# Expert rows transposed by a DMA on ScalarE's queue instead of on TensorE, and later issue of three experts' first weight loads

## The chip, the cores and the metric

One Trainium2 chip, one core of it. The metric is the device time of the whole program in microseconds; three runs of the kernel before gave 1927.49, 1928.22 and 1937.55, median 1928.22.

## The reference, cut to what matters

Two transformer layers over 2048 tokens of 512 features. The first has a latent attention and a mixture of experts, the second a memory attention and an MLP with a key-indexed expert table. Only the mixture of experts is touched by the change:

```python
h = x.reshape(T, d)                                   # 2048 x 512, normalized
scores = softmax(h @ gate_w.T)                        # 16 experts
topk_w, topk_idx = top_k(scores, 6)
cw = zeros((T, E)).at[arange(T)[:, None], topk_idx].add(topk_w)
for e in range(E):                                    # w_gate, w_up: 352 x 512, w_down: 512 x 352
    out = silu(h @ w_gate[e].T) * (h @ w_up[e].T) @ w_down[e].T
    y = y + cw[:, e:e + 1] * out
```

## The kernel before

Every fp32 product is made of three fp16 products (`mm3`, lines 234 to 236: high by high, high by low, low by high).

**Before the experts.** The attention runs for some 575 us. Beside it the kernel splits the expert weights into fp16 halves in DRAM (`wsp`), normalizes the 16 tiles of 128 tokens, stores each as a row table (`rows`, 2112 bytes a token: 512 high and 512 low halves and the 16 gate weights), stores the residual into `xacc`, and writes each token's number into the lists of its six experts (`recs`) with 96 indirect DMAs of GpSimd (L2226).

**The expert loop** runs over `NBLK` = 111 blocks of up to 128 tokens, each block of one expert. For block b:

- GpSimd gathers the block's 128 rows from `rows` into `xb[:, b % 6]` (`gather_rows`, L2298), `ROWS_AHEAD` = 5 blocks ahead: its loop is gather(b+5), then wait for `y_cp` of b and for `summed` of b-1, then the indirect DMA that adds the block's result to `xacc` (L2311). Since two of these could add to the same row, each waits until the one before it has landed.
- TensorE transposes the rows (`turn_rows`, 8 transposes of 128x128 fp16 into bank 4, L1061), ScalarE copies the bank to `xT[:, b % 2]` (`rows_copy`, L1468), and TensorE computes gate and up (`expert_up`, 24 matmuls of 352 columns).
- ScalarE takes the silu (L1474), VectorE multiplies (L2060), ScalarE and VectorE make the high and low halves (L1480, L2065), TensorE transposes them (`turn_hidden`, L1088), VectorE copies (L2072), TensorE computes the down product (`expert_down`, 9 matmuls of 512 columns), ScalarE scales it into one of `YB` = 3 buffers (`rows_out`, L1487) and increments `y_cp`. `rows_out` of b waits until the addition of b-3 has landed.
- TensorE's order in one turn of the loop is up(b+1), turn_rows(b+2), turn_hidden(b), down(b-1). ScalarE's is rows_out(b-2), silu(b+1), rows_copy(b+2), hidden_high(b+1).
- SyncE loads weights into four slots (`load_a`: 1408 KB gate and up, `load_d`: 768 KB down); at each block it issues a load that is carried out only where an expert is finished (L747, L755, with `cond`). It also reads the token lists, four blocks at a time (`records`, L714), and loads the memory for the next layer, 256 KB every third block (`memory_load`, L737).

**The start of the loop on SyncE** (L698 to L770): after the last head product it issues the gate and up weights of expert 0, the down weights of experts 0, 1 and 2, and, after the last attention product, the gate and up weights of expert 1. Then it waits for the tables, the stores of `xacc` and `rows`, and all 96 list writes (L759 to L764), reads the first list (L765) and the next seven (L714), and issues the rest of the first four experts' weights.

Of the kernel before, what the change touches and what calls it, by code (L numbers as in the profile page):

```python
# [10 lines left out]
ACT = mybir.ActivationFunctionType  # L11
# [35 lines left out]
XB, YB = 6, 3  # L47
REC_BATCH, REC_RING, ROWS_AHEAD = 4, 5, 5
# [11 lines left out]
def build(nc, ins, out):  # L60
    with ExitStack() as ctx:
# [3 lines left out]
        def sem(name):  # L65
            return ctx.enter_context(nc.semaphore(name))
# [388 lines left out]
        def pieces_of(m):  # L455
# [18 lines left out]
        xT = er2.take(2, 8 * P, dt=F16)  # L474
# [8 lines left out]
        assert er2.at <= xrow_at  # L483
        x_flat = x[:, :, :].rearrange("p a b -> p (a b)")
# [10 lines left out]
        xt_mm, xt_cp, e_g, e_u, e_sg, e_m, e_hh, e_hl, ht_mm, ht_cp, e_y, y_cp, e_cw = (  # L495
            sem(f"e_{what}") for what in ("xt_mm", "xt_cp", "g", "u", "sg", "m", "hh", "hl", "ht_mm", "ht_cp", "y",
# [123 lines left out]
        def _(sp):  # L620
# [79 lines left out]
            for e in range(SLOTS - 1):  # L700
                first_d(e)
            sp.wait_ge(y_mm, STEPS)
            first_a(1)
# [61 lines left out]
            sp.dma_start(rid[:, 0:1], recs[0:P, :]).then_inc(first_list, 16)  # L765
            records(0)
            records(1)
            first_a(2)
            first_d(3)
            first_a(3)  # L770
# [43 lines left out]
        def _(pe):  # L814
# [240 lines left out]
            def turn_rows(b):  # L1055
                pe.wait_ge(xb_in[b % XB], 16 * (b // XB + 1))
                if b > 0:
                    pe.wait_ge(xt_cp, b)
                o = bank[4][:, :].bitcast(F16)
                for i in range(8):  # L1060
                    m = pe.transpose(o[:, i * P:(i + 1) * P], xb[:, b % XB, i * P:(i + 1) * P], id16[:, :])  # L1061
                m.then_inc(xt_mm, 1)

# [3 lines left out]
            def expert_up(b, slot):  # L1067
                pe.wait_ge(xt_cp, b + 1)
                if b >= 2:
                    pe.wait_ge(e_m, b - 1)  # L1070
                pe.wait_ge(load_a[b % SLOTS], 16 * (b // SLOTS + 1))
                base = pe.snap(slot * (2 * AW))
                for i, done in ((0, e_g), (1, e_u)):
                    o = bank[2 * i + b % 2][:, 0:MOE_D]
                    for d in range(DC):
                        hi, lo = (wa[:, ds(base + (4 * d + 2 * k + i) * MOE_D, MOE_D)] for k in range(2))
                        m = mm3(pe, o, xT[:, b % 2, d * P:(d + 1) * P], xT[:, b % 2, (DC + d) * P:(DC + d + 1) * P],
                                hi, lo, start=(d == 0), stop=(d == DC - 1))
                    m.then_inc(done, 1)
# [27 lines left out]
            turn_rows(0)  # L1107
            turn_rows(1)
            expert_up(0, slots[0])
            for b in range(NBLK - 3):  # L1110
                expert_up(b + 1, slots[b + 1])
                slots[b + 2] = slot_of(b + 2)
                turn_rows(b + 2)
                turn_hidden(b)
                if b > 0:
                    expert_down(b - 1, slots.pop(b - 1))
# [3 lines left out]
            turn_rows(NBLK - 1)  # L1120
# [119 lines left out]
        def _(act):  # L1240
# [223 lines left out]
            def rows_copy(b):  # L1464
                act.wait_ge(xt_mm, b + 1)
                if b >= 2:
                    act.wait_ge(e_u, b - 1)
                act.activation(xT[:, b % 2, :], bank[4][:, :].bitcast(F16), ACT.Copy).then_inc(xt_cp, 1)  # L1468
# [21 lines left out]
            rows_copy(0)  # L1490
            rows_copy(1)
            expert_silu(0)
            hidden_high(0)
            for b in range(NBLK - 1):
# [5 lines left out]
                if b + 2 < NBLK:  # L1500
                    rows_copy(b + 2)
# [673 lines left out]
        def _(pool):  # L2175
# [111 lines left out]
            def gather_rows(b):  # L2287
# [7 lines left out]
                if b >= XB:  # L2295
                    pool.wait_ge(xt_mm, b - XB + 1)
                    pool.wait_ge(e_cw, b - XB + 1)
# [138 lines left out]
```

## Time and profile before

| | |
|---|---|
| median of three runs | 1928.22 us |
| the profiled execution, its own time | 1926.74 us |
| its span, first to last instruction | 1925.0 us |
| TensorE (PE) busy | 1801.6 us, 94% |
| VectorE (DVE), ScalarE (ACT), GpSimd (POOL) busy | 1093.7, 884.7, 820.2 us |
| mean granted TensorE clock | 0.977 |

The page gives busy time by engine, the span in forty slices, the DMA queues, and the chain of work that ended last. A busy share over the whole span says little here, since the program has stages with different limits; the expert loop lies between 606 and 1330 us. The time of a matmul in the profile is longer than its distance from the next one, as they are pipelined, so distances between starts are used where TensorE's pace matters. For a DMA the profile gives its issue on the engine and, for some, the time from issue to landing.

### The profile page before, as it was taken

What the parts mean: (1) busy time and instruction counts of PE and PEld (TensorE: products, weight loads), DVE (VectorE), ACT (ScalarE), POOL (GpSimd) and SP (SyncE); (2) the same over time, 40 slices, a digit from 0 to 9 for tenths busy, and PEclk for the clock granted to TensorE, in tenths of its full rate; (3) what the DMA queues carried; (4) which work ended last, traced back from release to release, by engine and by line L of the source; (5) the groups of instructions that cost most, each with busy time, mean ns of one, the idle gap of its engine ahead of it and who ended that gap; (6) DMA issues with size and microseconds to landing.
All of it is one profiled execution on the core that took longest, in us unless ns stands there. A gap on an engine that the chain in (4) does not pass through costs nothing.

```text
span 1925.0 us, 39526 instructions
## 1 busy us (share of the span) xinstructions
PE 1801.6 (94%) x12786; PEld 1073.8 (56%) x12789; DVE 1093.7 (57%) x2985; ACT 884.7 (46%) x1833; POOL 820.2 (43%) x731
## 2 busy tenths in 40 slices
PE   6989999999972999999999999995899999999998
PEld 3566666766631666666666666663554444444444
DVE  4578888888852323322322323223656877777776
ACT  4588888888841443444434434433732221122111
POOL 4234456656664344443433443442112444544442
PEclk9999999999985999999999999998999999999999
DMA  8255587777776666766665765545012355555653
GB/s 310 88 163 175 178 164 168 186 178 170 182 161 166 159 147 145 160 163 152 146 150 135 165 153 100 93 82 129 33 35 66 125 187 202 206 171 210 203 178 143
DMA packets 137921, 294.81 MB, mean 153 GB/s; under 512 B 39200, under 2 KB 64416, under 8 KB 133600
## 3 DMA queue, kind: packets, MB, share of 16 engines
q1 hardware_dynamic: 86752, 157.47, 29.5%
q0 software_dynamic: 46368, 126.29, 26.7%
q10 hardware_dynamic: 4608, 8.52, 1.5%
q8 instruction: 115, 1.88, 0.4%
q14 instruction: 78, 0.64, 0.1%
HBM read 426.00 MB, written 78.33 MB: 262 GB/s over the span
## 4 chain that ended last, share of the span: by engine, by line
PE 81%; DVE 6%; DMA 4%; issue 4%; ACT 3%; POOL 1%; SPq 0%; another core or an unknown queue 0%; ACTq 0%; POOLq 0%; DVEq 0%
PE bank L234 21%; PE bank L236 21%; PE bank L235 21%; PE bank L1061 3%; PE bank L1088 2%; PE bank L851 1%; DVE work_arena L1578 1%; DMA x_sum<-x,work_arena 1%; PE bank L927 1%; ACT xt_arena L1314 1%; PE bank L842 1%; POOL expert_tokens L2226 1%; DMA work_arena<-in_ctxT 1%; DMA work_arena<-in_pk_w 1%; DMA work_arena<-in_moe_w 1%
## 5 line engine op out<-in xcount | busy, mean ns | idle before, releaser
L234 PE MATMUL bank<-work_arena,xt_arena 128*128 x1221 | 404.7, 331 | 2.8 <-DVE xt_arena L2072 1.9
L235 PE MATMUL bank<-work_arena,xt_arena 128*128 x1221 | 404.6, 331 | 0.0
L236 PE MATMUL bank<-work_arena,xt_arena 128*128 x1221 | 404.5, 331 | 0.0
L2311 POOL DMA_INDIRECT x_sum<-x,work_arena x111 | 176.5, 1590 | 392.5 <-DMA x_sum<-x,work_arena 222.9
L2060 DVE TENSOR_TENSOR xt_arena<-xt_arena,bank 128x352 f32<-128x352 f32 x111 | 57.9, 522 | 405.9 <-PE bank L236 373.0
L234 PE MATMUL bank<-work_arena 128*128 128x512 f16 (+1 forms) x600 | 226.3, 378 | 15.1 <-DVE x L1883 6.8
L235 PE MATMUL bank<-work_arena 128*128 128x512 f16 (+1 forms) x600 | 226.4, 379 | 0.0
L236 PE MATMUL bank<-work_arena 128*128 128x512 f16 (+1 forms) x600 | 226.3, 378 | 0.0
L1468 ACT ACTIVATE xt_arena<-bank 128x1024 f16<-128x1024 f16 x111 | 113.6, 1023 | 224.4 <-PE bank L1061 212.0
L234 PE MATMUL bank<-xt_arena,work_arena 128*128 128x512 f16 x528 | 200.1, 379 | 1.7 <-DVE xt_arena L194 1.7
L235 PE MATMUL bank<-xt_arena,work_arena 128*128 128x512 f16 x528 | 200.1, 379 | 0.0
L236 PE MATMUL bank<-xt_arena,work_arena 128*128 128x512 f16 x528 | 200.1, 379 | 0.0
L2318 POOL TENSOR_TENSOR work_arena<-work_arena 128x512 f16<-128x512 f32 x64 | 73.3, 1164 | 267.7 <-ACT work_arena L1453 267.7
L236 PEld LDWEIGHTS bank<-work_arena,xt_arena 128*128 128x128 f16 x1221 | 119.7, 98 | 85.1
L234 PEld LDWEIGHTS bank<-work_arena,xt_arena 128*128 128x128 f16 x1221 | 119.8, 98 | 82.6 <-issue 3.3
L235 PEld LDWEIGHTS bank<-work_arena,xt_arena 128*128 128x128 f16 x1221 | 119.7, 98 | 79.4
L2327 POOL DMA_INDIRECT work_arena<-in_pk_e,work_arena x128 | 135.0, 1055 | 36.7 <-issue 33.4
L2298 POOL DMA_INDIRECT x<-token_rows,work_arena x111 | 112.0, 1009 | 49.7 <-issue 27.7
L1578 DVE SCALAR_TENSOR_TENSOR work_arena<-work_arena 128x704 f16<-128x704 f32 (+2 forms) x90 | 89.9, 1001 | 70.8 <-ACT work_arena L1361 54.1
L2212 POOL TENSOR_TENSOR xt_arena<-xt_arena,work_arena 128x512 f32<-128x512 f32 x64 | 66.8, 1043 | 137.0 <-DVE work_arena L1668 133.9
L1314 ACT ACTIVATE xt_arena<-xt_arena,work_arena 128x128 f32<-128x128 f32 x256 | 123.2, 482 | 2.1
L1487 ACT ACTIVATE x<-bank,xt_arena 128x512 f32<-128x512 f32 x111 | 76.3, 687 | 99.6 <-PE bank L236 92.6
(278 smaller groups left out, 3823.0 us busy)
## 6 DMA issues: line engine op xcount, KB each, us to landing
work_arena<-expert_w SPq DMA_DIRECT2D x111, 1408.0 KB
work_arena<-expert_w SPq DMA_DIRECT2D x111, 768.0 KB
work_arena<-in_moe_w SPq DMA_DIRECT2D x64, 352.0 KB
expert_w<-work_arena SPq DMA_DIRECT2D x64, 352.0 KB
work_arena<-in_moe_w SPq DMA_DIRECT2D x64, 192.0 KB
expert_w<-xt_arena SPq DMA_DIRECT2D x64, 192.0 KB
work_arena<-in_mlp_w SPq DMA_DIRECT2D x8, 1536.0 KB
work_arena<-in_head_w SPq DMA_DIRECT2D x16, 512.0 KB, 5.6
```

The costliest lines, as they stand in the source:

```text
L234: pe.matmul(o, a_hi, b_hi, start=start, stop=False)
L235: pe.matmul(o, a_hi, b_lo, start=False, stop=False)
L236: return pe.matmul(o, a_lo, b_hi, start=False, stop=stop)
L1314: last = act.activation(prob[:, m % 3, i, :], prob[:, m % 3, i, :], ACT.Exp, bias=ebias[:, m % 4, i:i + 1], scale=seg_scale[:, t:t + 1], a ...
L1468: act.activation(xT[:, b % 2, :], bank[4][:, :].bitcast(F16), ACT.Copy).then_inc(xt_cp, 1)
L1487: act.activation(ysb[:, b % YB, :], bank[6 + b % 2][:, :], ACT.Copy, scale=ecw[:, b % 4, :]).then_inc(y_cp, 1)
L1578: return dve.scalar_tensor_tensor(out=o, in0=src, scalar=scale, in1=hi, op0=ALU.mult, op1=ALU.subtract)
L2212: pool.tensor_tensor(prob[:, m % 3, :, :], prob[:, m % 3, :, :], rinv[:, m % 4, :].unsqueeze(2).to_broadcast([P, 4, P]), ALU.mult).then_in ...
L2298: pool.indirect_dma_start(out=xbu[:, b % XB, :], out_offset=None, in_=rows[:, :], in_offset=bass.IndirectOffsetOnAxis(ap=rid[:, i:i + 1], ...
L2311: pool.indirect_dma_start(out=xacc[:, :], out_offset=bass.IndirectOffsetOnAxis(ap=rid[:, i:i + 1], axis=0), in_=ysb[:, b % YB, :], in_offs ...
L2318: pool.tensor_tensor(h_lo[:, S_ % 2, c, :], m2[:, c, :], h_hi[:, S_ % 2, c, :], ALU.subtract).then_inc(hlo, 1)
L2327: pool.indirect_dma_start(out=gbuf[:, n % 2 * SETS + i - FIRST[n], :], out_offset=None, in_=ins["pk_e"][:, :], in_offset=bass.IndirectOffs ...
```

## The change

The eight transposes per block on TensorE and ScalarE's copy go. In their place ScalarE issues, for each block, one DMA that transposes the 128 x 1024 fp16 rows of `xb` into `xT` (256 KB, from SBUF to SBUF), three blocks ahead; `xT` has four buffers instead of two. ScalarE's instruction stream waits for the gather of that block (`xb_in`), for the up product that last read the buffer, and for the transposing DMA before the last one. TensorE waits for `xt_in` instead of `xt_cp`. In GpSimd's loop the gather waits for `xt_in` instead of `xt_mm`.

On SyncE only expert 0's weights (2176 KB) are issued ahead of the wait for the lists; experts 1, 2 and 3 follow behind the first list, between the further lists.

```diff
+XT_SLOTS, TURN_AHEAD = 4, 3
-        xT = er2.take(2, 8 * P, dt=F16)
+        xT = er2.take(XT_SLOTS, 8 * P, dt=F16)
...
             first_a(0)
-            for e in range(SLOTS - 1):
-                first_d(e)
-            sp.wait_ge(y_mm, STEPS)
-            first_a(1)
+            first_d(0)
...
             sp.dma_start(rid[:, 0:1], recs[0:P, :]).then_inc(first_list, 16)
+            first_a(1)
             records(0)
+            first_d(1)
+            first_a(2)
             records(1)
-            first_a(2)
+            first_d(2)
+            first_a(3)
             first_d(3)
-            first_a(3)
...
             def expert_up(b, slot):
-                pe.wait_ge(xt_cp, b + 1)
+                pe.wait_ge(xt_in[b % 2], 16 * (b // 2 + 1))
...
-            turn_rows(0)
-            turn_rows(1)
             expert_up(0, slots[0])
             for b in range(NBLK - 3):
                 expert_up(b + 1, slots[b + 1])
                 slots[b + 2] = slot_of(b + 2)
-                turn_rows(b + 2)
                 turn_hidden(b)
...
-            def rows_copy(b):
-                act.wait_ge(xt_mm, b + 1)
+            def rows_turned(b):
+                act.wait_ge(xb_in[b % XB], 16 * (b // XB + 1))
+                if b >= XT_SLOTS:
+                    act.wait_ge(e_u, b - XT_SLOTS + 1)
                 if b >= 2:
-                    act.wait_ge(e_u, b - 1)
-                act.activation(xT[:, b % 2, :], bank[4][:, :].bitcast(F16), ACT.Copy).then_inc(xt_cp, 1)
+                    act.wait_ge(xt_in[b % 2], 16 * (b // 2))
+                act.dma_start(xT[:, b % XT_SLOTS, :].rearrange("p (c r) -> p c r", c=8), xb[:, b % XB, 0:8 * P],
+                              transpose=True).then_inc(xt_in[b % 2], 16)
...
-            rows_copy(0)
-            rows_copy(1)
+            for b in range(TURN_AHEAD):
+                rows_turned(b)
...
                 expert_silu(b + 1)
-                if b + 2 < NBLK:
-                    rows_copy(b + 2)
+                if b + TURN_AHEAD < NBLK:
+                    rows_turned(b + TURN_AHEAD)
                 hidden_high(b + 1)
...
                 if b >= XB:
-                    pool.wait_ge(xt_mm, b - XB + 1)
+                    pool.wait_ge(xt_in[b % 2], 16 * ((b - XB) // 2 + 1))
                     pool.wait_ge(e_cw, b - XB + 1)
```

## Rows read from the trace of the kernel before

**Rows 1.** The page: span, and busy time of each engine.

```profile
span 1925.0 us, 39526 instructions
PE 1801.6 (94%) x12786; PEld 1073.8 (56%) x12789; DVE 1093.7 (57%) x2985; ACT 884.7 (46%) x1833; POOL 820.2 (43%) x731
```

**Rows 2.** A stretch: PE, PEld, DVE, ACT, POOL busy, clock, DMA share, GB/s.

```profile
700.00:800.00 100.00, 100.00 (x748) 63.61 (x747) 34.55 (x84) 40.63 (x64) 42.78 (x32) 1.00 0.67 150
```

**Rows 3.** Timeline of one block: start, duration, operation, [idle before, releaser].

```profile
900.71 0.46 ACT L1474 ACTIVATE xt_arena<-bank 128x352 f32<-128x352 f32 x1 [1.10 <-PE bank L236]
...
902.30 0.61 PE L1061 MATMUL bank<-id,x 128*128 128x128 f16 x8
...
902.75 0.50 PE L1088 MATMUL bank<-id,xt_arena 128*128 128x128 f16 x6
903.07 1.02 ACT L1468 ACTIVATE xt_arena<-bank 128x1024 f16<-128x1024 f16 x1 [1.90 <-PE bank L1061]
...
907.01 0.46 ACT L1474 ACTIVATE xt_arena<-bank 128x352 f32<-128x352 f32 x1 [1.10 <-issue]
```

**Rows 4.** The additions into x_sum, and what ended GpSimd's idle time before them.

```profile
L2311 POOL DMA_INDIRECT x_sum<-x,work_arena x111: 1541/1583/2516, 635.1 to 1325.0; - x111
  DMA x_sum<-x,work_arena: 222.9, 66
  ACT x L1487: 146.5, 41
DMA to landing us min/median/max: 3.7/4.9/11.9
```

**Rows 5.** Timeline of GpSimd: the first addition and three later ones.

```profile
635.11 1.63 POOL L2311 DMA_INDIRECT x_sum<-x,work_arena  x1 [14.16 <-ACT x L1487]
...
654.02 1.57 POOL L2311 DMA_INDIRECT x_sum<-x,work_arena  x1 [3.43 <-ACT x L1487]
...
663.40 1.60 POOL L2311 DMA_INDIRECT x_sum<-x,work_arena  x1 [6.51 <-issue]
...
668.91 1.59 POOL L2311 DMA_INDIRECT x_sum<-x,work_arena  x1 [2.62 <-DMA x_sum<-x,work_arena]
```

**Rows 6.** Weight load, memory load; landings of the additions of 1183.57 and 1189.87.

```profile
653.09 0.35 SPq L747 DMA_DIRECT2D work_arena<-expert_w  x1
...
1183.56 0.62 SPq L737 DMA_DIRECT2D work_arena<-in_ctxT  x1
DMA to landing us min/median/max: 5.4/5.4/5.4
...
DMA to landing us min/median/max: 4.8/4.8/4.8
```

**Rows 7.** Stretches between additions: memory load, none, memory load (columns as Rows 2).

```profile
1183.57:1189.87 6.30, 6.30 (x49) 4.01 (x47) 1.86 (x5) 2.56 (x4) 2.56 (x2) 1.00 0.60 127
1189.87:1196.18 6.31, 6.31 (x49) 4.01 (x47) 1.86 (x5) 2.56 (x4) 2.57 (x3) 1.00 0.46 87
...
1202.48:1208.79 6.31, 6.31 (x49) 4.01 (x47) 1.86 (x5) 2.56 (x4) 2.57 (x3) 1.00 0.66 130
```

**Rows 8.** Waits of SyncE's queue, then the timeline of the loop's start.

```profile
SPq L763 <- DMA token_rows<-xt_arena: 29.1, 1, 29.1
594.89 0.97 POOL L2226 DMA_INDIRECT expert_tokens<-work_arena  x1 [0.30 <-issue]
606.14 0.34 SPq L765 DMA_DIRECT2D work_arena<-expert_tokens  x1
612.35 0.97 POOL L2298 DMA_INDIRECT x<-token_rows,work_arena  x1 [1.21 <-DMA work_arena<-expert_tokens]
613.58 1.03 PE L1061 MATMUL bank<-id,x 128*128 128x128 f16 x8 [20.97 <-DMA x<-token_rows,work_arena]
615.82 1.01 PE L1061 MATMUL bank<-id,x 128*128 128x128 f16 x8 [1.21 <-DMA x<-token_rows,work_arena]
616.63 0.50 PE L234 MATMUL bank<-work_arena,xt_arena 128*128 x1
```

More of the change, by code:

```diff
@@ L483, in build @@
         assert er2.at <= xrow_at
+        er2.at = (er2.at + 7) // 8 * 8
+        xT = er2.take(XT_SLOTS, 8 * P, dt=F16)
         x_flat = x[:, :, :].rearrange("p a b -> p (a b)")
@@ L494, in build @@
         xb_in = [sem(f"xb_in{s}") for s in range(XB)]
-        xt_mm, xt_cp, e_g, e_u, e_sg, e_m, e_hh, e_hl, ht_mm, ht_cp, e_y, y_cp, e_cw = (
-            sem(f"e_{what}") for what in ("xt_mm", "xt_cp", "g", "u", "sg", "m", "hh", "hl", "ht_mm", "ht_cp", "y",
+        xt_in = [sem(f"xt_in{s}") for s in range(2)]
+        e_g, e_u, e_sg, e_m, e_hh, e_hl, ht_mm, ht_cp, e_y, y_cp, e_cw = (
+            sem(f"e_{what}") for what in ("g", "u", "sg", "m", "hh", "hl", "ht_mm", "ht_cp", "y",
                                           "y_cp", "cw"))
@@ L1053, in _ @@
             last.then_inc(q_mm, 1)
[L1055 to L1062, printed above, removed]
             def slot_of(b):
@@ L1076, in expert_up @@
                         hi, lo = (wa[:, ds(base + (4 * d + 2 * k + i) * MOE_D, MOE_D)] for k in range(2))
-                        m = mm3(pe, o, xT[:, b % 2, d * P:(d + 1) * P], xT[:, b % 2, (DC + d) * P:(DC + d + 1) * P],
+                        m = mm3(pe, o, xT[:, b % XT_SLOTS, d * P:(d + 1) * P],
+                                xT[:, b % XT_SLOTS, (DC + d) * P:(DC + d + 1) * P],
                                 hi, lo, start=(d == 0), stop=(d == DC - 1))
@@ L1119, in _ @@
             slots[NBLK - 1] = slot_of(NBLK - 1)
-            turn_rows(NBLK - 1)
             turn_hidden(NBLK - 3)
```

## The prediction

> **What bounds the kernel now.** I read the page first, for the shares [rows 1]; then the busy time by stretch, since the shares are a mean over stages; then one block of the expert loop in the timeline; then, because the change adds traffic, the waits and landings of the other chain that runs block by block, GpSimd's additions. TensorE is busy for 94% of the span, and in the loop it never stops: 100.00 us of 100 at a granted clock of 1.00, the 2.4 GHz level, while the DMA engines are at 0.67 [rows 2]. One block lasts from one silu to the next, 900.71 to 907.01, 6.30 us [rows 3]. So TensorE sets the loop's pace, and what the change takes off TensorE seems to be a gain in full.
>
> The reader should look at who is second. The additions into x_sum follow each other one at a time, each waiting for the landing of the last. The first is issued at 635.1 and the last at 1325.0: 110 intervals in 689.9 us, a mean of 6.27. Of GpSimd's idle times before them 66 were ended by the landing of the addition before (with 4 more put down to others), 41 by ScalarE's result [rows 4]. In well over half of the blocks the chain of additions, not TensorE, is the later of the two. It is elastic: it falls behind when a weight load is carried out and catches up after. Behind the load issued at 653.09 the interval from 654.02 to 663.40 is 9.38 us, and the next, 663.40 to 668.91, is 5.51 [rows 5, 6]. In that interval GpSimd was idle for 2.62, so its own work (this issue, its gaps and the next gather) is 5.51 - 2.62 = 2.89 us. About 5.5 us is the chain's floor: a landing of 4.9 [rows 4] and some 0.6 from there to the next issue.
>
> **The change part by part.**
>
> *TensorE loses eight transposes per block.* Their first starts at 902.30 and the next work at 902.75, 0.45 us, so a block would take 6.30 - 0.45 = 5.85 us [rows 3]; over 111 blocks 50 us. ScalarE's copy of 1.02 us goes too [rows 3]; ScalarE's four instructions take 2.66 us of 6.30, so this frees nothing on the path.
>
> *What is late next: the additions.* How fast can that chain go as it is? The 41 waits ended by ScalarE sum to 146.5 us [rows 4]; without the first, 14.16 [rows 5], they are 132.3 over 40 intervals, and with 2.86 of work each these 40 last 247 us. At the floor of 5.5 they would last 220. So with TensorE infinitely fast the additions still need 689.9 - 27 = 663 us. Of the 50 us at most 27 can come through, and that is with nothing added to the chain.
>
> *What a transposing DMA adds to it.* It moves 256 KB a block on the same 16 engines. No DMA here transposes. The nearest rows are the memory loads, also 256 KB, issued by an engine's hardware queue. The one at 1183.56 goes out with the addition of 1183.57: that addition lands after 5.4 us, the next, with no load beside it, after 4.8 [rows 6], so 0.6 us more; the DMA share of the stretches is 0.60 and 0.66 with such a load and 0.46 without, that is 0.14 x 6.3 = 0.9 to 0.20 x 6.3 = 1.3 us of all 16 engines per transfer [rows 7]. From below the bound is zero: an addition's transfer can be over before the other starts. A gain is excluded, since nothing is taken off the DMA engines. From above it is the whole 1.3 us. The phase decides. Once the additions are behind, ScalarE at its transposing DMA of block b+3 waits for the gather of b+3, which GpSimd issues 1.9 us after addition b-3; a gather took 615.82 - 612.35 = 3.47 us to its user [rows 8], which makes 5.4 after that addition, right where the next is issued. That is the phase of the row with 0.6 and not that of a load that falls between two. I take 0.45, nearer to that row than to zero, since a copy within SBUF doesn't read DRAM. The chain then needs 663 + 110 x 0.45 = 712.5 us against 689.9: +23 us. It breaks even at 27 / 110 = 0.24 us per block.
>
> Here the Trainium skill speaks for the change: Advanced Engine Details and Errata, X-Bar Transpose (TRN2), says that transposing DMAs run about as fast as plain ones, at 350 to 400 GB/s. An estimate from it is 262144 B / 375 GB/s = 0.7 us of all engines, a little under the rows' 0.9 to 1.3; scaling the 0.6 us by it gives 0.4 us a block and a chain of 663 + 44 = 707 us, +17.
>
> *ScalarE's queue.* Behind a DMA whose gather is late stand hidden_high and the next rows_out. The copy starts at 903.07, and TensorE transposes the hidden halves that follow it one block after 902.75, at 909.05 [rows 3]; the copy's 1.02 us and two halves of about 0.5 us lie between, which leaves more than 3 us, so waits up to that are covered. An ordinary 256 KB issue takes 0.36 to 0.62 us of a queue [rows 6]; if a transposing one takes up to the 3.6 us that ScalarE has free (6.30 - 2.66), the block is still covered. `xt_in` instead of `xt_mm` in GpSimd's loop concerns a block six back: nothing. The doubled `xT` costs nothing. With expert loads in flight the transposing DMA shares the engines with them and lands late too; it is issued more than a block, 5.8 us, before its user, which covers a delay like the 3.9 us of 9.38 against 5.5.
>
> *The start.* The last list write is issued at 594.89, the first list read only at 606.14; SyncE waited for the store of the row table [rows 8]. Some 2.9 MB of weights (768 + 768 + 1408 KB) were in front. If writes land in 3 us, the list can be read at 598: -8 us at most. Against it: these loads now run beside the first gathers and transposes, and records stand behind 1408 KB. From 606.14 to the first up product it is 10.5 us; the first gather's user starts at 613.58 and the two PE transposes and copies end at 616.63, 3.05 us, which the first transposing DMA takes over at about the same price [rows 8]. Beside a weight load an addition took 3.9 more; I take 2.5 for the gather and 2.5 for the transposing DMA. -8 + 5 = -3 us, bounds -8 and +5.
>
> *The sum*, against the profiled time of 1926.74: +23 - 3 = +20, 1946.7. The median of the runs is 1.5 above that execution: 1948.
>
> **The rivals.**
>
> 1. *TensorE's gain comes through*: the transposing DMA falls into the pause between two additions, as after 1.9 us of GpSimd's own work, when no transfer of it is in flight. Between 0 and 0.19 us a block; the chain needs 663 to 684, the loop gains 27 to 6, the start 3 to 8. About 1928 - 20 - 6 = 1902. For it: the pause is some 2 us long and the added transfer 0.9 to 1.3. Against: the phase above.
> 2. *They cancel*: 0.19 to 0.37 us a block; 1919 to 1938, about 1928.
> 3. *The additions are slowed by 0.45*, the forecast, 1938 to 1965: the other side of rival 1, one mechanism, deciding from 0.24 us on.
> 4. *The DMA engines fill up*. Now 0.67 x 6.3 = 4.2 us of 16 engines a block in the stretch with loads [rows 2]; if a transposing transfer takes 2.7 us, twice the costlier memory load, a block needs 6.9 us there, and with some 90 such blocks +55 us, and queueing on top: 1980 to 2020. It decides from 6.3 - 4.2 = 2.1 us on. No row shows a 256 KB transfer that slow.
> 5. *The transposing DMA doesn't pipeline*: its queue handles it in pieces, eight of 128 x 128, and it takes longer than a block. Each piece at 1.2 us, the cost of a whole memory load, gives 9.6 us a block, 111 x 3.3 = +366 us, 2290. Against it: all 256 KB transfers here take a tenth of that. The Trainium skill has a rule of this kind, against the change: VectorE: DVE Perf Modes, The three transpose paths, gives 1309 ns for one 128x128 by DMA against 390 on TensorE and advises TensorE; eight in a row would make, as an estimate, 10.5 us a block and 2390. Its 390 ns is not what this trace shows on TensorE, 0.45 us for all eight [rows 3].
>
> **How the numbers follow.** Rival 1: 0.27. Rival 2: 0.18. Forecast 3: 0.35. Rival 4: 0.13. Rival 5: 0.07. A difference under 0.5%, 9.6 us, can't be told from no change here. So faster 0.27, same 0.18, slower 0.55. The time is that of case 3, 1948, whose own range is 1938 to 1965. The range for 8 in 10 goes down to 1898, leaving out a little of rival 1, and up to 2020, leaving out rival 5.
>
> **What would show it.** In the profile after: no L1061; 24 + 6 + 9 matmuls a block with gaps between them, TensorE below 100 of 100 in the loop; nearly all of GpSimd's idle time before L2311 ended by the landing of x_sum, ScalarE's share of it almost gone; quiet intervals near 6.0 instead of 5.5; a landing median of about 5.3 instead of 4.9; the DMA share of the loop above 0.8; the first list read near 598. I'd be wrong if the landing stays at 4.9 and TensorE is still full (rival 1), if the DMA share is at 1 (rival 4), or if ScalarE's queue shows issues of several microseconds or TensorE waits for `xT` in every block (rival 5).

## The result and the profile after

The changed kernel takes 1997.13 us (median of 4 runs, 1984.20 to 2009.36) against 1929.74 us for the kernel before on the same chip: 1.034 times as long, 95% interval 1.030 to 1.038. The forecast was 1948 us, so the sign was right and the rise was over three times as large as forecast, +67 us instead of +20. The four executions lie 25 us apart, those of the kernel before 10 us, and the profiled one is the fastest of the four, 1984.20 us.

The page of the changed kernel: span, busy times, DMA queues, two parts of the chain that ended last, and the two groups of additions and first products.

```profile
span 1982.4 us, 37643 instructions
PE 1775.6 (90%) x11901; PEld 1026.3 (52%) x11901; DVE 1084.7 (55%) x2985; ACT 770.1 (39%) x1722; POOL 820.3 (41%) x731
...
q1 hardware_dynamic: 86752, 157.47, 28.8%
q0 software_dynamic: 46368, 126.29, 26.2%
q10 hardware_dynamic: 121824, 37.63, 11.5%
...
PE 43%; DMA 32%; issue 9%; DVE 7%; ACT 4%; POOL 2%; SPq 1%; another core or an unknown queue 1%; ACTq 1%; POOLq 0%; DVEq 0%
...
L235 PE MATMUL bank<-work_arena,xt_arena 128*128 x1221 | 411.2, 337 | 95.7 <-DMA xt_arena<-x 93.3
```

TensorE is busy for 26 us less [rows 1] and yet the span is 57 us longer. A third of the chain that ended last is now DMA time. The queue q10, ScalarE's, carried 4608 packets in the kernel before, all but a few of them ahead of the loop; with the transposing DMAs it carries 121824 and takes 11.5% of the DMA engines' span.

The stretch of [rows 2], three more of the loop, and its greater part (PE, PEld, DVE, ACT, POOL busy, clock, DMA share, GB/s):

```profile
640.00:1180.00 540.00, 480.39 (x3066) 282.67 (x3064) 144.79 (x398) 118.28 (x236) 199.46 (x154) 0.97 0.88 176
700.00:800.00 100.00, 91.54 (x582) 53.54 (x583) 31.60 (x79) 21.65 (x46) 38.26 (x30) 0.98 0.86 182
800.00:900.00 100.00, 84.32 (x531) 49.37 (x530) 25.43 (x72) 22.22 (x44) 36.90 (x29) 0.94 0.89 182
1100.00:1200.00 100.00, 85.17 (x545) 50.35 (x544) 24.83 (x70) 21.64 (x42) 35.04 (x28) 0.95 1.00 174
1200.00:1300.00 100.00, 99.25 (x661) 60.00 (x659) 30.12 (x85) 26.53 (x51) 43.65 (x34) 1.00 0.83 145
```

GpSimd issues twice per block, a gather and an addition. From 1200 on, where few weights are loaded, x34 makes 17 blocks in 100 us, 5.9 us each: faster than before's 6.3, as the change intends. Between 800 and 900 x29 makes 14.5 blocks, 6.9 us each, and from 1100 to 1200, with 7.1 us a block, the times of all packets add up to all of the 16 engines' time (share 1.00). In the queue's row of that stretch 3.67 MB are 14 transposing DMAs, and they took 37.0 us of 16 engines, 2.64 us each:

```profile
q10 hardware_dynamic: 14761, 3.67, 37.0%
```

The additions into x_sum, as [rows 4], and the transposing DMA: issue durations, first and last start, who waited.

```profile
L2305 POOL DMA_INDIRECT x_sum<-x,work_arena x111: 1541/1583/1627, 647.1 to 1380.5; - x111
  DMA x_sum<-x,work_arena: 323.5, 84
  ACT x L1481: 41.0, 6
DMA to landing us min/median/max: 3.9/5.3/12.0
...
L1461 ACTq DMA_TRANSPOSE xt_arena<-x x111: 1247/1252/6562, 616.6 to 1353.2; - x111
  PE bank L235: 93.3, 25
```

84 waits for the landing of the addition before instead of 66, 6 for ScalarE instead of 41: the chain of additions has taken TensorE's place. Where a wait is for several things at once, the profile can name the wrong one, so I also set each addition beside the landing of the one before and the end of ScalarE's result for it. In the changed kernel the landing came last in 97 of 110 intervals, in the kernel before in 70. The profiled executions differ in three terms. The first addition comes at 647.1 instead of 635.1: +12. The loop takes 1380.5 - 647.1 = 733.4 us instead of 689.9: +43.5. What follows takes 601.9 instead of 600.0: +2. Together +57.5, and the median lies another 10 or so above.

### The profile page after: what moved, and what is told of

It is laid out like the page before. It is cut to its first block, busy times and chain, and to the rows that moved or that the text cites. A ratio compares the mean times of both kernels' runs of the same rounds, so it can differ in the third digit from the quotient of the medians.

```text
span 1982.4 us, 37643 instructions
## 1 busy us (share of the span) xinstructions
PE 1775.6 (90%) x11901; PEld 1026.3 (52%) x11901; DVE 1084.7 (55%) x2985; ACT 770.1 (39%) x1722; POOL 820.3 (41%) x731
## 3 DMA queue, kind: packets, MB, share of 16 engines
q1 hardware_dynamic: 86752, 157.47, 28.8%
q10 hardware_dynamic: 121824, 37.63, 11.5%
## 4 chain that ended last, share of the span: by engine, by line
PE 43%; DMA 32%; issue 9%; DVE 7%; ACT 4%; POOL 2%; SPq 1%; another core or an unknown queue 1%; ACTq 1%; POOLq 0%; DVEq 0%
DMA x_sum<-x,work_arena 25%; PE bank L235 11%; PE bank L237 11%; PE bank L236 11%; DMA x<-token_rows,work_arena 3%; DVE work_arena L1572 2%; PE bank L854 1%; DMA xt_arena<-x 1%; ACT xt_arena L1305 1%; PE bank L930 1%; DMA expert_w<-work_arena 1%; PE bank L845 1%; POOL expert_tokens L2220 1%; DMA work_arena<-in_pk_w 1%; DVE xt_arena L1572 1%
## 5 line engine op out<-in xcount | busy, mean ns | idle before, releaser
L235 PE MATMUL bank<-work_arena,xt_arena 128*128 x1221 | 411.2, 337 | 95.7 <-DMA xt_arena<-x 93.3
L236 PE MATMUL bank<-work_arena,xt_arena 128*128 x1221 | 410.6, 336 | 0.0
L237 PE MATMUL bank<-work_arena,xt_arena 128*128 x1221 | 410.2, 336 | 0.0
L1474 ACT ACTIVATE xt_arena<-xt_arena 128x352 f16<-128x352 f32 x111 | 55.1, 496 | 470.9 <-issue 399.6
L235 PEld LDWEIGHTS bank<-work_arena,xt_arena 128*128 128x128 f16 x1221 | 121.3, 99 | 192.0 <-issue 112.8
L2059 DVE TENSOR_TENSOR xt_arena<-xt_arena 128x352 f16<-128x352 f32 x111 | 58.3, 525 | 294.4 <-ACT xt_arena L1474 283.2
L237 PEld LDWEIGHTS bank<-work_arena,xt_arena 128*128 128x128 f16 x1221 | 121.5, 99 | 84.1
L236 PEld LDWEIGHTS bank<-work_arena,xt_arena 128*128 128x128 f16 x1221 | 121.2, 99 | 80.2 <-issue 0.4
```

Source lines behind the costliest of these rows:

```text
L235: pe.matmul(o, a_hi, b_hi, start=start, stop=False)
L236: pe.matmul(o, a_hi, b_lo, start=False, stop=False)
L237: return pe.matmul(o, a_lo, b_hi, start=False, stop=stop)
L2059: dve.tensor_tensor(eh_lo[:, b % 2, 0:MOE_D], em[:, b % 2, :], eh_hi[:, b % 2, 0:MOE_D], ALU.subtract).then_inc(e_hl, 1)
```

## The experiments

Ratios are to runs of the kernel before on the same chip in the same comparison, with the 95% interval; times are medians. "+" lines of an edit are cut to the core. A loop is the time from the first addition's issue to the last one's, 689.9 us before.

**The changed kernel again.** No edit.

> The changed kernel itself, for comparison with the others of this set: 1.030 to 1.040, with executions as far apart as before, some 25 us.

2003.73 us, 1.040 [1.036, 1.043]. The size holds: +3.4 to +4.0% in two comparisons. Its profiled execution is one of the long ones, 2011.3 us span, with a loop of 761.3 us instead of 733.4, the mean granted clock at 0.956 and TensorE's waits for the turned rows in the loop at 75.5 us.

**The start.** The changed kernel with the old order of weight loads, and the kernel before with the new one.

```diff
-            first_d(0)
+            for e in range(SLOTS - 1):
+                first_d(e)
+            sp.wait_ge(y_mm, STEPS)
+            first_a(1)
```

> The changed kernel with the old order of the first weight loads on SyncE (three down loads and expert 1's up load ahead of the lists). In the changed kernel the first list is read at 601.4 instead of 606.1, but the first up product starts at 629.9 instead of 616.6, since the first three transposing DMAs take 14.4 us to issue beside the weight loads. Theory start (the loads moved behind the list delay the first transposing DMAs): first up product at 617 to 621 and 9 to 13 us less in total, about 1985 against the changed kernel's median of 1997. Rival (the transposing DMA is slow by itself, loads or not): first up product still near 630 and the total within 3 us of 1997.

> The kernel before with only the new order of the first weight loads; transposes stay on TensorE. Theory start: without transposing DMAs the order costs little, the first list is read at about 601 and the first up product starts between 612 and 618; the total is 1922 to 1932 against 1930. Rival (the weight loads behind the list delay the gathers themselves): first up product at 620 or later and 1935 or more.

2005.39 us, 1.033 [1.024, 1.042], and 1926.75 us, 1.002 [1.000, 1.004]. The order of loads by itself does nothing to the time: its first list is read at 600.08, but its first product starts at 618.50, 1.9 us later than before. In the changed kernel undoing it makes no difference that the scatter would let through. What the start costs is seen in the timeline of the changed kernel (start, duration, operation, [idle before, releaser]):

```profile
593.14 0.97 POOL L2220 DMA_INDIRECT expert_tokens<-work_arena  x1 [0.30 <-issue]
...
601.41 0.34 SPq L765 DMA_DIRECT2D work_arena<-expert_tokens  x1
...
607.76 2.64 POOL L2292 DMA_INDIRECT x<-token_rows,work_arena  x1 [13.65 <-DMA work_arena<-expert_tokens]
...
616.62 14.43 ACTq L1461 DMA_TRANSPOSE xt_arena<-x  x3
...
629.86 0.47 PE L235 MATMUL bank<-work_arena,xt_arena 128*128 x1 [38.99 <-DMA xt_arena<-x]
```

The list is read 4.7 us earlier (601.41 against 606.14, [rows 8]), and the first product starts 13.2 us later (629.86 against 616.63). Between them stand 14.43 us from ScalarE's first transposing DMA to the end of its third. With the old order the three take as long, but the first product starts at 612.51, before the later rows are turned:

```profile
606.73 16.21 ACTq L1461 DMA_TRANSPOSE xt_arena<-x  x3
```

These rows merge three instructions and the waits between them. Taken apart, the changed kernel's three issues, and those of the spare plain copy in runs of 256 B described below (shortest, median and longest, first and last start):

```profile
L1461 ACTq DMA_TRANSPOSE xt_arena<-x x3: 1248/1422/6562, 616.6 to 629.8; - x3
...
L1498 ACTq DMA_DIRECT2D xt_arena<-x x3: 602/685/853, 619.3 to 633.9; - x3
```

The third may go out only when the first has landed. The first transposing DMA landed at 629.7, 13.1 us after its issue, and then both the third goes out and the first product starts. The plain copy landed 14.5 us after its issue. So the one issue of 6.56 us is peculiar to the transposing DMA, but not the late landing, which decides when the first product starts.

**Is the chain of additions the bound?** The additions alternate between two sums in DRAM, so that each waits for the one before the last; once in the changed kernel, once in the kernel before with one transpose per block in place of eight, and that one also with a single sum. None of the three computes the reference: the second sum is left out of the output, and with one transpose most of `xT` keeps the rows of the first two blocks.

```diff
-                for i in range(8):
+                for i in range(8 if b < 2 else 1):
...
-                if b > 0:
-                    pool.wait_ge(summed, 16 * b)
+                if b > 1:
+                    pool.wait_ge(summed[b % 2], 16 * (b // 2))
...
+                    out=(xacc, xacc_b)[b % 2][:, :], out_offset=bass.IndirectOffsetOnAxis(ap=rid[:, i:i + 1], axis=0),
```

> The changed kernel with the additions of even and odd blocks going to two different sums, each addition waiting for the one before the last; the second sum is left out of the output. This takes the chain of additions off the path and leaves all traffic. Theory additions (the forecast's: the chain of additions is the bound): the waits of TensorE for xT mostly go too, the loop falls from 733 to 680 to 695 us and the total to 1945 to 1960. Theory late rows (transposing DMAs land late beside weight loads, TensorE waits for xT, and ScalarE's queue waits behind them): TensorE still waits 70 us or more for xT and the total stays above 1980.

> The kernel before with one transpose of the eight and a copy of 128 columns in every block from the third on (the rest of xT keeps the rows of the first two blocks, so the output is another). No transposing DMA, no added traffic. The forecast's step: the additions let through at most 27 of TensorE's 50 us. So 1895 to 1905 against 1926. Rival (the chain of additions has no say while TensorE is faster): TensorE's 0.39 us times 109 in full, 1880 to 1886.

> The same with the additions of even and odd blocks going to two sums (the second is left out of the output), so that each waits for the one before the last. If the additions are what holds the kernel with one transpose back, this one gains the rest: 1878 to 1888. If both are equal, the chain of additions was not the bound.

One transpose: 1916.89 us, 0.993 [0.990, 0.995]. One transpose and two sums: 1886.26 us, 0.976 [0.973, 0.980]. The changed kernel with two sums: 1955.70 us, 1.018 [1.013, 1.024], its four executions from 1928.49 to 1964.66, so that its size is known roughly only. The kernel with one transpose, its additions and a wait in its loop:

```profile
L2312 POOL DMA_INDIRECT x_sum<-x,work_arena x111: 1541/1583/1927, 633.6 to 1317.3; - x111
  DMA x_sum<-x,work_arena: 251.8, 75
  ACT x L1488: 90.9, 25
...
PEld bank L1061 <- DMA x<-token_rows,work_arena: 27.2, 18, 4.3
```

Seven of eight transposes are 44 us by the forecast's price. With two sums 46 us come through (1932.18 - 1886.26), so that price is right. With one sum it is 15. The loop falls from 689.9 to 683.7 us only, and in the loop TensorE now waits for gathered rows, which it never did before: a late addition holds up the gather that GpSimd issues behind it. The chain of additions is the bound as soon as TensorE gets faster. (Two sums in the kernel before with all eight transposes weren't run; TensorE is busy for 100 us of 100 there.)

The 25 waits put down to ScalarE mislead here. The k-th of ScalarE's results (L1488) belongs to the k-th addition. The addition of 856.70 uses the result of 849.54, which was ready 6.5 us earlier. The addition before it, of 851.00, landed after 4.9 us, and 0.8 us later the next went out:

```profile
849.54 0.69 ACT L1488 ACTIVATE x<-bank,xt_arena 128x512 f32<-128x512 f32 x1 [1.22 <-PE bank L236]
851.00 1.58 POOL L2312 DMA_INDIRECT x_sum<-x,work_arena  x1 [2.95 <-ACT x L1488]
855.46 0.69 ACT L1488 ACTIVATE x<-bank,xt_arena 128x512 f32<-128x512 f32 x1 [1.23 <-DMA x_sum<-x,work_arena]
856.70 1.58 POOL L2312 DMA_INDIRECT x_sum<-x,work_arena  x1 [2.83 <-ACT x L1488]
...
DMA to landing us min/median/max: 4.9/4.9/4.9
```

Set beside each other in this way, the landing came last in 108 of the 110 intervals. The whole loop of 683.7 us is the chain: 595.6 us of landings, 87.1 us from a landing to the next issue (0.77 us in most), and 1.0 us of waiting for ScalarE.

In the changed kernel the two sums give back some 31 to 42 us (1.018 against 1.034 and 1.040), and more by its fastest execution. Behind them the next limits stand (windows of that execution, columns as above):

```profile
800.00:900.00 100.00, 98.07 (x653) 59.06 (x651) 29.10 (x82) 26.06 (x50) 42.51 (x33) 1.00 1.02 208
1000.00:1100.00 100.00, 97.23 (x635) 58.25 (x633) 28.88 (x83) 26.50 (x50) 42.38 (x33) 0.98 1.00 186
```

At 6.1 us a block the DMA share is 1.00 and TensorE is busy for 97 to 98 us of 100; TensorE alone would need 5.85.

**The wait or the traffic?** The kernel before, with ScalarE waiting for the gather of block b+3 and nothing else; then with an unused DMA of the gathered rows per block in the changed kernel's place, which transposes, copies in runs of 256 B, or copies in runs of 2048 B. Besides, ScalarE waits for the spare DMA before the last, as in the changed kernel, and GpSimd's gather for that of six blocks back; the kernel with the wait alone has neither.

```diff
+            def rows_spare(b):
+                act.wait_ge(xb_in[b % XB], 16 * (b // XB + 1))
...
+                act.dma_start(spareT[:, b % 4, :].rearrange("p (c r) -> p c r", c=8), xb[:, b % XB, 0:8 * P],
+                              transpose=True).then_inc(spare_in[b % 2], 16)
```

> The kernel before with only the wait of the change in ScalarE's stream: before hidden_high it waits for the gather of three blocks ahead; no DMA is added. Theory queue (ScalarE's waiting in order for a gather that is issued behind a late addition costs time by itself): 1940 or more, with 200 us or more of ScalarE's idle time ended by the gather. Theory contention: the wait alone costs under 5 us, 1924 to 1931, since TensorE has slack for the hidden halves.

> The kernel before (transposes on TensorE, old start) with one transposing DMA per block added on ScalarE's queue, at the same place as in the changed kernel, into a spare buffer that nobody reads. Pure added traffic and queue time, no gain. Theory contention (the transposing DMA makes the additions and gathers late, whoever uses its result): the total is 1970 to 2010, as in the changed kernel, and the landing median of the additions 5.3 to 5.7. Theory late rows (a large part of the loss is TensorE waiting for xT): the total is 1935 to 1960.

> The same as the kernel with the spare transposing DMA, but the spare DMA is a plain copy of the same 256 KB in runs of 256 bytes. Theory packets (the cost is the 1024 packets of 256 bytes, some 25 ns each on an engine): within 10 us of the kernel with the spare transposing DMA. Rival (the transposition itself is what costs): under 1940.

> The same with the plain copy in runs of 2048 bytes, 128 packets. Theory packets: some 0.7 us of 16 engines a block instead of 1.6; the forecast's own kind of transfer. With TensorE still doing the transposes the additions have 27 us of room over the loop, so the total is 1925 to 1940. Rival (bytes are what counts): as with 256-byte runs, 1960 or more.

| added to the kernel before | us | ratio | loop, us | per block | of 16 engines, each |
|---|---|---|---|---|---|
| wait alone | 1932.06 | 1.000 [0.998, 1.001] | | | |
| copy, 2048 B runs | 1960.30 | 1.019 [1.017, 1.021] | 717.8 | +0.25 | 0.73 us |
| copy, 256 B runs | 1969.40 | 1.021 [1.018, 1.023] | 722.6 | +0.30 | 1.2 us |
| transposing DMA | 2009.83 | 1.042 [1.038, 1.047] | 741.7 | +0.47 | 1.90 us |

"Per block" is the loop's growth over 110 intervals, in the profiled execution. For the transposing DMA that is the fastest of six (1984.37 us), for the copies the fastest (2048 B) and the slowest (256 B) of five, so the last row's +0.47 is low beside its median. The last column comes from the DMA queues in the stretch 1200 to 1300: the share of 100 us over the transfers in it, which are 16 by their bytes and 15.5 for the transposing DMA; q10 of the three kernels in the table's order of copies, then the transposing one:

```profile
q10 hardware_dynamic: 2304, 4.20, 11.7%
```

```profile
q10 hardware_dynamic: 16656, 4.20, 19.5%
```

```profile
q10 hardware_dynamic: 16356, 4.07, 29.5%
```

The wait for the gather costs nothing. Any 256 KB beside the chain, with the waits that come with it, costs about 2% (the expectation for runs of 2048 B was under 1%), and that the rows are transposed on the way doubles it: at the same bytes and nearly the same packets (16656 and 16356) the packets take half as long again, and the issue takes a median of 1.25 us of ScalarE's queue instead of 0.60, and 10.5 us at worst:

```profile
L1498 ACTq DMA_TRANSPOSE xt_arena<-x x111: 1247/1249/10547, 610.5 to 1359.4; - x111
```

The landings of the additions grow nearly alike: 638.2 us over the loop with the transposing DMA, 630.5 and 625.6 with the copies in runs of 256 and 2048 B, 583.3 before. What differs more is TensorE's wait for the hidden halves, the first of which ScalarE makes behind its DMA. With the transposing DMA and with the copy in runs of 256 B, in the loop:

```profile
PE bank L1092 <- DVE xt_arena L2080: 28.8, 26, 2.7
```

```profile
PE bank L1092 <- DVE xt_arena L2079: 14.4, 14, 1.2
```

It is 13.6 us with runs of 2048 B and 1.7 with the wait alone. So of the 19 us between the first two loops 8 go with longer landings and 14 with ScalarE's late halves; the two overlap in part, and neither was changed by itself.

**Half of it.** The same spare DMA with 128 KB; and a working mixture, in which TensorE turns the high halves (four transposes) and a DMA the low halves.

```diff
+                act.dma_start(spareT[:, b % 4, 0:4 * P].rearrange("p (c r) -> p c r", c=4), xb[:, b % XB, 0:4 * P],
+                              transpose=True).then_inc(spare_in[b % 2], 16)
```

> The kernel before with a spare transposing DMA of 128 KB per block, half of the full one. If engine time is the cost, it is like the plain copy of 256 KB in runs of 2048 bytes, which takes about as much engine time: ratio 1.012 to 1.022. If the transposition costs beyond its engine time (the half change with TensorE's saving gave 1.028): 1.028 to 1.040.

> The kernel before with half of the change: the high halves are transposed by TensorE (4 transposes, a copy of 512 columns), the low halves by a transposing DMA of 128 KB three blocks ahead; old start. TensorE saves 0.22 us a block, 25 us. Theory additions: the chain has 27 us of room and the half transfer costs it about half of the full one; 1920 to 1945. Theory late rows: TensorE waits for the low halves beside each weight load, 1955 or more.

1969.74 us, 1.024 [1.020, 1.028], and 1977.62 us, 1.028 [1.026, 1.030]. Half the bytes cost 2.4%, which is about half of the whole's 4.2 or a little more, and lies between the two ranges expected. The mixture gains nothing over the spare: 25 us less of TensorE's work (half of the 50) don't show.

**Where no weights are in flight.** Transposing DMAs for the last 21 blocks only.

```diff
+                if b >= LATE:
+                    return
```

> The kernel before with the change's transposing DMAs for the last 21 blocks only, where hardly any weight load is left; old start. In the changed kernel the intervals between additions there are 5.5 to 6.5 us, some 5.95 in the mean, against 6.30 before. If the additions' floor plus 0.3 to 0.4 us per transposing DMA holds: a gain of 4 to 9 us, 1917 to 1922. If the transposing DMA costs its 0.64 us a block here too: 1926 or slower.

1930.96 us, 0.999 [0.996, 1.002], loop 686.5 us. The 4 to 9 us of gain that were expected don't show beyond the scatter; the loop is 3.4 us shorter. Where the DMA engines were at about half, the change costs nothing. The loss is made beside the weight loads.

**Shorter runs of the weight loads.** Those loads in runs of 1408 and 1536 B (q1 then has 107232 packets instead of 86752), in the changed kernel and in the kernel with the spare transposing DMA.

```diff
+                             max_dma_last_dim=1408).then_inc(load_a[e], 16)
...
+                             max_dma_last_dim=1536).then_inc(load_d[e], 16)
```

> The changed kernel with the expert weight loads cut into runs of 1408 and 1536 bytes instead of rows of 11264 and 6144 bytes; same bytes, same order. Theory packets in turn (a DMA engine takes packets of the queues in turn, so that a transposing DMA's 256-byte packets each wait for one of 11264 bytes): the intervals of 11 us between additions beside a weight load fall to 8 or 9, TensorE's wait for xT from 93 us to under 40, the first three transposing DMAs issue in under 8 us instead of 14.4, and the total falls by 20 to 45 us, to 1950 to 1975. Rival (bytes, not packets, are what is shared): nothing changes by more than 5 us, or it is slower for the smaller runs.

> The kernel before with the spare transposing DMA of 256 KB per block, and the expert weight loads in runs of 1408 and 1536 bytes. If what makes the transposing DMA cost twice the plain copy (1.042 against 1.0205) is its packets' waiting behind long weight packets: 1.020 to 1.030. If it is its own time on the engines or the way it goes through them: 1.036 to 1.045.

1977.43 us, 1.024 [1.017, 1.031], and 1996.98 us, 1.034 [1.030, 1.038]. Both lie below the kernels without the edit: the first by 1.0 to 1.6 of a per cent (1.034 and 1.040), the second by 0.8 (1.042). The intervals overlap or touch, but for that against 1.040. That the long runs of the weights hold up the others may be a fifth to two fifths of the cost; it isn't the main part. The transposing DMA itself took no less of the engines: 1.9 us between 640 and 1180 with the spare one, with and without the edit.

**The lead.** The changed kernel with the rows turned two blocks ahead instead of three.

```diff
-XT_SLOTS, TURN_AHEAD = 4, 3
+XT_SLOTS, TURN_AHEAD = 4, 2
```

> The changed kernel with TURN_AHEAD = 2 instead of 3: ScalarE no longer waits for the gather three blocks ahead, but the transposing DMA has a block less until its user. Theory late rows: TensorE's wait for xT grows from 93 us to 150 or more and the total by 10 to 30 us. Theory queue: ScalarE's waits fall and the total falls by 10 us or more. Theory additions and traffic: within 8 us of the changed kernel in the same set of runs.

2133.51 us, 1.107 [1.103, 1.110]: 130 us over the changed kernel. Its transposing DMA with who waited, its additions with what ended GpSimd's idle time, and one window:

```profile
  PE bank L235: 212.4, 82
...
L2305 POOL DMA_INDIRECT x_sum<-x,work_arena x111: 1541/1583/1627, 649.1 to 1532.5; - x111
  ACT x L1481: 498.3, 89
  DMA x_sum<-x,work_arena: 74.2, 17
...
640.00:1180.00 540.00, 426.99 (x2567) 244.47 (x2566) 122.01 (x334) 108.04 (x197) 166.84 (x130) 0.93 0.74 145
```

TensorE waits in 82 blocks instead of 25, for 212 us instead of 93, and the additions wait for its results 89 times. The DMA share falls to 0.74, so full engines aren't the reason here: one block less of lead no longer covers the transfer. Issued behind the silu of b+1, it has less than a block until TensorE's up product of b+2. In its chain of waits one such transfer reads

```profile
796.87 5.75 DMA xt_arena<-x
```

5.75 us, nearly a block. The changed kernel with the old order, in a long execution, has the landings of all 111:

```profile
DMA to landing us min/median/max: 2.7/5.3/23.5
```

The granted clock of the stretch is 0.93; the mean product of line 235 took 351 ns in it, 337 in the changed kernel, 331 before. The loss against the changed kernel, expected at 10 to 30 us, came out at more than four times the upper end.

No kernel with a transposing DMA that computes the reference was faster than the kernel before.

## Why the prediction was right or wrong

*TensorE's gain, 0.45 us a block:* right. With the chain of additions out of the way, seven transposes less gave 46 us, 44 by the forecast's price.

*The additions' floor, 663 us:* this step failed. That the additions bound the loop once TensorE is faster was right, and even more so than forecast; the size of their floor was wrong. The one-transpose kernel measured 683.7, with the landing last in 108 of 110 intervals. The forecast replaced each of the 40 intervals that ended with ScalarE by the quiet 5.5 us, a landing of 4.9 and 0.6. From a landing to the next issue it takes 0.77 in most, and not every landing is a quiet one. With the kernel before's own landings, 583.3 us, and the 87.1 between them the floor is 670; the one-transpose kernel's landings took 12 us more. Why they did wasn't tested, and kernels without added traffic differ as much among themselves (586.5 with the new order, 595.9 with the wait alone). Only some 6 of the 27 us appear in the loop, 15 in the median. So there was far less gain to set against the cost. This is 20 us of the error of 47.

*0.45 us a block for the transposing DMA:* the size held in the fastest execution, its grounds did not. Against the measured floor the changed loop pays (733.4 - 683.7) / 110 = 0.45 us, and the landings alone (642.4 instead of 595.6 us) 0.43 an addition. The spare transposing DMA costs 0.47 beside the kernel before. But in the long execution of 2011.3 us the same sum gives (761.3 - 683.7) / 110 = 0.71, so the median execution lies somewhat above 0.45. The forecast had its value from memory loads in the belief that the transfer takes 0.9 to 1.3 us of the engines. It took 1.64 in the changed kernel from 1200 to 1300 (27.8% of 100 us for 17) and 2.64 from 1100 to 1200, and 1.90 beside the kernel before. A plain copy of the same bytes, which is what the rows of memory loads were nearest to, costs 0.25 to 0.30. The value of 0.45 was thus partly luck.

The Trainium skill (Advanced Engine Details and Errata, X-Bar Transpose (TRN2)) says that transposing DMAs run about as fast as plain ones, at 350 to 400 GB/s. Here they don't: 262144 B in 1.64 to 1.90 us of all engines is 138 to 160 GB/s, and the plain copy with 2048 B runs took 0.73 us, 359 GB/s. The measurement decides; by the page the cost per block should have been nearer to the copy's. The Trainium skill's page VectorE: DVE Perf Modes (Rules for kernel authors) advises TensorE for a 128x128 transpose that may go to PSUM, and the result agrees; the 1309 ns of its section The three transpose paths for one 128x128 by DMA, times eight, does not fit the 1.64 to 2.64 us of all engines that eight took here.

*ScalarE's queue:* half right. The added wait for the gather costs nothing, as the wait-only kernel shows. The issue was said to be covered up to 3.6 us; its median is 1.25, but single ones took up to 6.56 us, and in the loop TensorE waited in 13 blocks for hidden halves, 12.3 us in all. (15 of GpSimd's waits are put down to VectorE's L2047, but the addition waits for no result of VectorE.) An example is this burst in the changed kernel, after the weight load of 796.72:

```profile
796.72 0.35 SPq L747 DMA_DIRECT2D work_arena<-expert_w  x1
...
797.90 1.67 ACTq L1461 DMA_TRANSPOSE xt_arena<-x  x1
...
808.44 1.58 POOL L2305 DMA_INDIRECT x_sum<-x,work_arena  x1 [7.95 <-DMA x_sum<-x,work_arena]
809.97 0.47 PE L235 MATMUL bank<-work_arena,xt_arena 128*128 x1 [6.37 <-DMA xt_arena<-x]
```

The addition before was issued at 797.62, so this interval is 10.8 us, and TensorE stood for 6.37 in it. Before, the longest such interval in [rows 5] was 9.38, and TensorE never stood. The step "issued more than a block before its user, which covers a delay like the 3.9 us" was wrong in 24 blocks of the loop, 54 us in all, and at the start, where TensorE waits for 39.0 us instead of 20.97 for its first rows.

*The start, -3 us (bounds -8 and +5):* wrong in sign, +12 in the trace. The earlier list came (4.7 us, not 8). The added term was priced at one delay of 2.5 us each for a gather and a transposing DMA. From the list's read to the first product the changed kernel needs 28.45 us instead of 10.49. Up to the first gather's issue it is 6.35 instead of 2.36, since the list itself now lands beside weight loads. From there to its user it is 8.86 instead of 5.08. The first transposing DMA then takes 13.24 until the first product starts, where two transposes and copies took 3.05. The error is 15 us, and half of it is that last term, priced at 5.55.

*What is left:* 20 and 15 us of the error of 47 are named, 2 lie behind the loop, and about 10 are the distance from the profiled execution to the median. The long executions have a lower mean granted clock (0.956 at a span of 2011.3, 0.963 at 1982.4), longer landings of the additions (670.5 us against 642.4) and longer waits for the turned rows (75.5 us against 51.1 between 650 and 1300). Which of the three comes first, the runs don't tell.

*The rivals.* Rivals 1 and 2 fell with the first median, and rival 5 with transfers of 1.6 to 2.6 us of the engines: TensorE waited for them in 25 blocks, not in 111. Rival 4, full DMA engines at 1980 to 2020, has the time, and half of the mechanism. Its price of 2.7 us a transfer came between 1100 and 1200 (2.64, at a share of 1.00); from 640 to 1180 it is 1.8 and the mean share 0.88. As soon as the additions' chain is split the share is 0.99 over the same 540 us. The forecast's mechanism and rival 4's act together: the chain is slowed and, where weights are loaded, there is little left for it to catch up in.

*The signs:* L1061 gone, TensorE below 100 of 100, idle times ended by the landing of x_sum, landing median 5.3, quiet blocks of 5.9 us, share above 0.8: all as forecast. The list read at 601 and not at 598.

*What stays open:* why turning the rows on the way costs twice what moving them does. Longer packet times (1.90 against 1.2 us), longer issues and TensorE's waits for hidden halves (28.8 against 14.4 us) go with it, and shorter weight runs take back two fifths at most. Why the transposing DMA's time on the engines goes from 1.6 to 2.6 us between stretches, where a plain copy's stays at 1.2, is open too. Whether the additions and gathers are held up by the engines' time alone or by something the queues share wasn't told apart. Nor was it tried to issue the transposing DMA from another engine's queue, or weight loads apart from it in time.

## What to carry to other kernels

Before work is taken off the engine that is busy at 100%, measure how much of it can come through: a kernel that leaves the work out, run beside one with the second chain relaxed, tells it in two runs; here it was 15 and 46 us. A chain of waits has its floor not in its quiet intervals but in the sum of its landings, slow ones too, and of the time from each landing to the next issue. Where the profile names another engine as the end of such a wait, compare times: a result that was ready 6 us earlier ended nothing. A DMA that replaces engine work is to be priced by a spare one in the old kernel, for its traffic, its issue and its lead separately, above all where weight loads leave the DMA engines under a third of their time.

## What the runs showed of the hardware

- 256 KB within SBUF took 0.73 us of all 16 DMA engines in 2048 B runs, 1.2 us in 256 B runs, and transposed (1056 packets) 1.64 us in one stretch of the changed kernel and 2.64 in another.
- Issuing a transposing DMA held ScalarE's queue for 1.25 us in the median against 0.47 to 0.60 us for plain ones, and for up to 6.6 to 10.5 us beside weight loads; the longest issue of a plain copy there took 0.85 us. The first to go out took 13.1 us to land, a plain copy at the same place 14.5.
- One transposing DMA took 5.75 us to its user (median to landing 5.3 in another kernel), and with two blocks of lead the kernel took 130 us more than with three.
- A plain spare copy per block, which TensorE doesn't wait for, cost 2%: the landings of the accumulating DMAs took 625.6 to 630.5 us in the loop instead of 583.3.
- In a chain of accumulating indirect DMAs the next one was issued 0.77 us after the landing in most intervals, with quiet landings of 4.7 to 5.0 us.
- The granted clock was 0.94 in a stretch in which TensorE was busy 84 of 100 us with gaps of up to 6.4 us, and 1.00 where it was busy 99 of 100.
